# Scores of four heads at once in the last layers of a four-layer cross-attention kernel, and another order on GpSimd in its first layer

## What is computed

```python
q = q.reshape(b, l, KVH, GROUPS, HD).transpose(0, 2, 3, 1, 4)
scores = jnp.einsum('bkgld,bksd->bkgls', q, k) * scale
scores = scores + encoder_attention_mask[:, :, None, :, :]
attn = jax.nn.softmax(scores, axis=-1)
out = jnp.einsum('bkgls,bksd->bkgld', attn, v)
```

## Time and profile before

| | us |
|---|---|
| median of 3 runs | 1202.15 (1202.07 to 1203.07) |
| the profiled execution | 1202.93 |
| its span | 1200.9 |
| granted TensorE clock, mean over the span | 0.983 of full speed |
| layer 0, about | 0 to 702 |
| layer 1, about | 720 to 889 |
| last layers: first turn, last turn | 909.6, 1185.1 |

### The profile page before, as it was taken

How to read it: one execution, slowest core, us unless ns; L and a number is a source line. 1 busy time by engine, 2 the same in 40 slices (tenths; PEclk the granted TensorE clock), 3 DMA queues, 4 the chain that set the end, 5 groups by cost and what they waited for, 6 DMA issues and landing times. The chain is left out here.

```text
span 1200.9 us, 20667 instructions
## 1 busy us (share of the span) xinstructions
PE 1118.7 (93%) x7404; PEld 883.7 (74%) x7404; DVE 808.3 (67%) x1986; ACT 646.7 (54%) x1451; POOL 684.2 (57%) x746
## 2 busy tenths in 40 slices
PE   5999999999999999999999988989689999999996
PEld 4888788988898888898878973444456767667674
DVE  6677666686667766767765757688656655666774
ACT  3655655656556555655565211622235656687764
POOL 3666665675656656656676303476016655565874
PEclk9899999999999999999999997999799999999999
DMA  6101210221022102210220300000020100000000
GB/s 212 55 25 65 71 53 19 71 71 53 19 71 71 54 18 71 71 54 19 71 71 19 93 5 13 1 1 0 1 62 2 37 1 2 1 2 1 11 10 19
DMA packets 35338, 46.97 MB, mean 39 GB/s; under 512 B 3931, under 2 KB 22308, under 8 KB 35237
## 3 DMA queue, kind: packets, MB, share of 16 engines
q1 hardware_dynamic: 34866, 45.00, 11.6%
q10 hardware_dynamic: 370, 0.64, 0.2%
HBM read 44.59 MB, written 1.05 MB: 38 GB/s over the span
## 5 line engine op out<-in xcount | busy, mean ns | idle before, releaser
L379 POOL TENSOR_TENSOR a_prob<-a_prob,a_inv_total 128x512 f32<-128x512 f32 x128 | 144.2, 1126 | 192.4 <-DVE a_inv_total L684 192.4
L2027 POOL TENSOR_TENSOR scores<-scores,neg_max 128x512 f32<-128x512 f32 x144 | 147.5, 1041 | 79.5 <-DVE neg_max L1898 79.3
L574 ACT ACTIVATE a_prob<-psum,a_neg_max 128x257 f32<-128x257 f32 x256 | 119.2, 472 | 101.7 <-DVE a_neg_max L681 100.4
L1821 ACT ACTIVATE prob_T<-psum 128x512 f32<-128x512 f32 x192 | 113.1, 600 | 35.5 <-PE psum L1742 34.0
L1742 PE MATMUL psum<-ident,scores 128*128 128x128 f32 x768 | 117.8, 280 | 1.5 <-POOL scores L2027 1.5
L1742 PEld LDWEIGHTS psum<-ident,scores 128*128 128x128 f32 x768 | 85.7, 141 | 36.8 <-issue 16.3
L1898 DVE CUSTOM_DVE_ANT_0 scores<-psum,ctx_rows 128x256 f32<-128x256 f32 x256 | 93.7, 420 | 18.6 <-PE psum L1742 9.2
L688 DVE TENSOR_TENSOR a_probT_lo<-psum,a_probT_hi 128x512 fp32r<-128x512 f32 x128 | 88.0, 687 | 24.3 <-ACT a_probT_hi L578 24.0
L503 PE MATMUL psum<-ident,a_prob 128*128 128x128 f32 x512 | 77.3, 273 | 14.6 <-POOL rows_bc L383 12.6
L681 DVE TENSOR_REDUCE a_neg_max<-psum 128x2 f32<-128x514 f32 x128 | 87.4, 683 | 1.2 <-PE psum L425 1.2
L503 PEld LDWEIGHTS psum<-ident,a_prob 128*128 128x128 f32 x512 | 60.6, 140 | 32.7 <-DVE a_q_lo L730 13.4
(11 more groups left out here) (358 smaller groups left out, 3319.1 us busy)
## 6 DMA issues: line engine op xcount, KB each, us to landing
wk_raw<-in_L_xattn_wk SPq DMA_DIRECT2D x16, 512.0 KB, 6.3
wq_raw<-in_L_xattn_wq SPq DMA_DIRECT2D x16, 512.0 KB, 5.6
wv_raw<-in_L_xattn_wv SPq DMA_DIRECT2D x16, 512.0 KB, 3.7
wo_raw<-in_L_xattn_wo SPq DMA_DIRECT2D x16, 512.0 KB, 4.0
ctx_rows<-in_ctx SPq DMA_DIRECT2D x3, 512.0 KB, 4.2
x_rows<-in_x SPq DMA_DIRECT2D x2, 512.0 KB, 9.9
ctx_rows<-in_mask_Bx1xSxS_ff SPq DMA_DIRECT2D x1, 1024.0 KB, 5.4
out_dram<-x_rows SPq DMA_DIRECT2D x4, 256.0 KB, 2.1
```

Source lines behind the costliest of these rows:

```text
L379: pool.tensor_tensor(prob[:, m % 4, :, 0:S], prob[:, m % 4, :, 0:S], rtot[:, m % 4, :].unsqueeze(2).to_broadcast([P, 2, S]), ALU.mult)
L574: act.activation(prob[:, m % 4, q, 0:S + 1], s_bank(g)[:, q, 0:S + 1], ACT.Exp, bias=negm[:, m % 4, q:q + 1], accum_out=tot[:, m % 4, q:q ...
L1821: act.activation(pT[:, i % PT, :], t_bank(i), ACT.Exp, scale=1.0 if on_scalar(i) else -1.0).then_inc(exp_ok, 1)
L2027: pool.tensor_tensor(sc[:, i % SC, :, :], sc[:, i % SC, :, :], m[:, i % SC, :].unsqueeze(2).to_broadcast([P, 2, S]), ALU.subtract).then_in ...
```

## The change

- A call of `scores` does the four heads of a quad, in four row groups and four banks. It is issued two quads ahead (`LEAD` = 2), after the turn of each head with i % 4 == 1, and waits until all heads of the quad before have been read by DVE.
- The sums of two quads stand in a row, after every eighth head; for that the probabilities have ten slots instead of eight, and `exp` waits accordingly.
- The values of layer 2 stand 17 columns apart instead of 32; the matmul still loads 32 columns, the last 15 of which belong to the next head. 15 zero columns close each row, and the memset is narrower.
- DVE takes one more maximum ahead of the eviction of a piece behind an odd turn.
- In layer 0, GpSimd does `norm(6)` and `norm(7)` ahead of the wait for V3 and the cut of the value weights in iterations with i % 4 of 1 and 2.

```diff
                     if i % NQ == 2:
                         h_low(event_of(i))
+                    if i % NQ in (1, 2):
+                        norm(6)
+                        norm(7)
                     pool.wait_ge(acc_full, USE[i, 'V3'] + 1)
                     cut_half('v', i + 1, 0)
-                    norm(6)
+                    if i % NQ not in (1, 2):
+                        norm(6)
                     cut_half('v', i + 1, 1)
-                    norm(7)
+                    if i % NQ not in (1, 2):
+                        norm(7)
...
-LEAD = 4
+LEAD = 2
...
-    pe = [('F', p) for p in opening] + [('S', 0), ('S', 1)] + [('F', p) for p in second] + [('S', 2), ('S', 3)]
+    pe = [('F', p) for p in opening] + [('S', 0)] + [('F', p) for p in second] + [('S', 1)]
     for i in range(HEADS):
         pe.append(('T', i))
         if i in behind:
             pe.append(('F', behind[i]))
-        if i % 2 and i // 2 + LEAD < HEADS // 2:
-            pe.append(('S', i // 2 + LEAD))
-        if i % 4 == 1 and i > 4:
-            pe.append(('A', i // 4 - 1))
-    pe += [('A', QUADS - 1)] + [('F', p) for p in ending]
+        if i % 4 == 1 and i // 4 + LEAD < QUADS:
+            pe.append(('S', i // 4 + LEAD))
+        if i % 8 == 1 and i > 8:
+            pe += [('A', i // 4 - 2), ('A', i // 4 - 1)]
+    pe += [('A', QUADS - 2), ('A', QUADS - 1)] + [('F', p) for p in ending]
...
-                    max_to(at + (5 if at % 2 else 6))
+                    max_to(at + 6)
...
-        v_ones2 = sb("v_ones", [P, 2, 4, SMALL[2].KV, 32])
+        v_ones2 = sb("v_ones", [P, 2, 4, SMALL[2].KV * 17 + 15])
...
-        SC, PT = 7, 8
+        SC, PT = 7, 10
...
-        v_ones = {(2, h): v_ones2[:, h] for h in range(2)}
+        v_ones = {(2, h): v_ones2[:, h, :, 0:SMALL[2].KV * 17].rearrange("p t (k e) -> p t k e", e=17) for h in range(2)}
+        v_cols = lambda l, h, t, k: v_ones2[:, h, t, 17 * k:17 * k + 32] if l == 2 else v_ones[l, h][:, t, k, :]
...
-                    l, b, e = head_of(2 * s)
+                    l, b, e = head_of(4 * s)
...
-                    if s >= 2:
-                        pe.wait_ge(s_read, 2 * s - 2)
+                    if s:
+                        pe.wait_ge(s_read, 4 * s)
...
-                            for i in (2 * s, 2 * s + 1):
+                            for i in range(4 * s, 4 * s + 4):
...
                     if i >= PT:
-                        act.wait_ge(a_done, i // 4 - 1)
+                        act.wait_ge(a_done, (i - PT) // 4 + 1)
...
-                    dve.wait_ge(s_full, i // 2 + 1)
+                    dve.wait_ge(s_full, i // 4 + 1)
```

More of the change, by code:

```diff
@@ L1462, in last_layers_orders @@
     for kind, p in pe:
-        if kind == 'S' and p == 2:
+        if kind == 'S' and p == 1:
             act.append(('shift', 2))
@@ L1469, in last_layers_orders @@
             act.append(('keep', p))
-            if p == QUADS - 1:
+            if p == QUADS - 2:
                 at = HEADS
@@ L1713, in scores @@
                 def scores(s):
-                    l, b, e = head_of(2 * s)
+                    l, b, e = head_of(4 * s)
                     sh = SMALL[l]
-                    if s < 2:
+                    if s == 0:
                         pieces = [p for (kind, p), bank in bank_of.items() if kind == 'F' and bank < 4]
                         landed(pe, [max((p for p in pieces if evictor(p) == who), key=number.get) for who in ('act', 'dve')])
-                    if e % 4 == 0 and b % 2 == 0:
+                    if b % 2 == 0:
                         landed(pe, stack_pieces(l, b // 2, e // 4))
-                    if s >= 2:
-                        pe.wait_ge(s_read, 2 * s - 2)
+                    if s:
+                        pe.wait_ge(s_read, 4 * s)
                     at = b % 2 * S
@@ L1756, in sums @@
                             j = i % 4
-                            mm = pe.matmul(a_bank(n)[rows(j), :], v_ones[l, b // 2][:, b % 2 * 2 + t, (e + j) * SMALL[l].KV // SMALL[l].H, :],
+                            mm = pe.matmul(a_bank(n)[rows(j), :], v_cols(l, b // 2, b % 2 * 2 + t, (e + j) * SMALL[l].KV // SMALL[l].H),
                                            pT[:, i % PT, t * S:(t + 1) * S], start=t == 0, stop=t == 1, tile_position=(0, 32 * j))
@@ L1968, in set_ones @@
                     W = SMALL[l].W
-                    pool.memset(v_ones[l, h][:, :, :, W + 1:32], 0.0)
+                    pool.memset(v_ones2[:, h, :, SMALL[2].KV * 17:] if l == 2 else v_ones[l, h][:, :, :, W + 1:32], 0.0)
                     return pool.memset(v_ones[l, h][:, :, :, W:W + 1], 1.0)
```

## The result

The changed kernel takes 1213.43 us in the median of five runs (1212.70 to 1214.76), the kernel before 1202.07 (1200.32 to 1203.07): a ratio of 1.0099, with a 95% interval of 1.0085 to 1.0112, so 11.4 us slower. The forecast was 1205.4, 3.3 slower; the time has its sign and lies in the whole range of 1188 to 1217, but above the 1200 to 1211 that the forecast gave its own mechanism, and the loss is over three times as large as forecast. By the time alone rival B (1211 to 1216) and rival D (1213) would fit too. The question is thus which term was too small.

The account below looks back on a forecast made before the run. PE (TensorE) was taken as the bound, busy 93% of the span. 1202.9 - 7.5 (layer 0) + 9.6 (last layers) + 1.2 (clock) = 1206.2, less 0.8 for the median: 1205.4 us; own range 1200 to 1211, whole 1188 to 1217.

Parts of the forecast that it names:

- rival B: Last layers: half clock costs 1.7 after each of four waits over 2 us, less after nine; 1211 to 1216; chance 0.12.
- rival D: Layer 0: moving GpSimd's normalisations gains nothing; 1213 us; chance 0.10.
- Layer 0: GpSimd's norm(7) ahead of the cuts brings turn T7 1.9 us earlier in four iterations: -7.5 us, bounds 0 and -10.
- What PE no longer does: Last layers: one of two score blocks per quad goes, 29.2 us, paired sums save 5.5: -34.7, plus 0.6 for four-head blocks.
- rival C: Score blocks: row groups run only two at a time, +13 us, 1218 us; chance 0.07.
- The pairs of sums: Last layers: two sum blocks in a row take 1.81, not 2 x 1.00; 0.25 for each of 22 pairs, 5.5 us.
- The waits: Last layers: PE's score blocks of quads 3 to 47 wait for DVE's late maxima, +50.6 us in sum.
- the walk: Last layers: step times of PE and DVE added quad by quad, by slots and order; the layers' sum is +9.6 us.
- The single prices: Score block's wait per quad: 1.15 us plain, 1.55 with one 'OT' piece, 2.9 behind layer 3's projection and moments.
- Rival A: Last layers: only a quad's last maximum is late, wait 0.65 instead of 1.55, 14 us less: 1191 us; chance 0.15.
- the clock: Last layers: four new waits over 2 us can each bring PE to half clock; 0 to 7 us, taken as 1.2.
- The end: From head 182 on, GpSimd's normalisation no longer holds PE up and the last quad's exponential hides behind sums: -2.4 us.

Follow-up runs that it names:

- four blocks later: The changed kernel with only the score blocks of quads 19, 22, 41 and 45 issued one turn later: 1209.40 us, ratio 1.0069 to the kernel before.

## Why the prediction came out as it did

**Layer 0** was right in size and place: 7.5 us forecast, 7.5 measured; T7's time, the unchanged i % 4 == 1 and the cover of about 1 us ahead of norm(0) came as said. Of its signs one came only in part: T7 still waits 0.4 us for GpSimd in two of the four iterations. Rival D (nothing) has the measured time, 1213, but the run with this part alone puts it out.

**What PE no longer does.** The score block of four costs what a pair costs, so rival C is out. The pairs of sums were mis-sized: 0.25 us each was forecast and 0.14 measured, 2.4 us too much for 22 pairs. The pair itself was taken at 1.81 and takes 1.87; the slow turn that was to go with it brought nothing that the traces show.

**The waits.** 50.6 were forecast. The table has 43.8, and 1.0 more at one block that waits for an 'OB' eviction on ScalarE. That is 5.8 less. Some 2.6 of it is the way of counting: the table counts from the modelled end of the last matmul (1127.60 + 1.47 = 1129.07), the walk from the step, 0.07 earlier (1126.67 + 2.33), in 37 places. Another 1.4 was taken by the half clock: the blocks of quads 42 and 46, right behind a stretch, wait 0.13 and 0.54, and 1.05 and 1.06 in the kernel with eight slots, which has no stretch there. The last 1.8 isn't placed. The single prices (1.15, 1.55, 2.9) are met within 0.03 in the table (1.14, 1.52, 2.88). Rival A (only the last maximum late, 0.65 at an 'OT' quad) is out by the 1.52.

**The reason for the waits was half right.** The prediction's first sentence on it says that the slot is free too late. But at an 'OT' quad the three maxima stand behind the eviction in VectorE's written order, and that is the later of the two: an eighth slot took away 2.2 of 44.5 us of waits, nine slots without the order left 39.2, and nine with it 1.7. The walk held both conditions, so its numbers came out; the sentence named only one, and someone who had acted on it would have bought a slot and gained 4.5 us, where the order was worth 31.

**The term that was mis-sized most is the clock.** I took 1.2 us for it, on the ground that VectorE is late anyway while PE runs at half clock, and that only the four waits over 2 us count. Measured are four stretches that cost 5.5 by the walk; between traces, the two in quads 19 to 23 are worth 2.8 and the two in quads 42 to 46 1.8, 4.6 together. The ground was wrong in both halves. VectorE's lateness covers part of a stretch at best: in the second pair 1.4 of 3.2 us of added busy time, as the waits of quads 42 and 46 show, and in the first pair none that shows. And the size of a wait doesn't decide: those of 2.34 in quad 3 and of 2.88 in quad 34 brought none, those of 1.84 and 1.90 in quads 19 and 22 did. Rival B gave the time, 1211 to 1216, with this mechanism, though not with the waits that it named; its 0.12 was too little. That the time came into the whole range is thus owed to the room left for a rival, not to the forecast's own sum.

The rest of the difference: some 3 us are steps that the walk had too short, 2.4 of them the pairs of sums and 0.9 quad 12, ahead of whose block a transposed input and the projection Q behind it wait 0.50 and 0.49 for evictions before them (at 975.26 and 976.81; the second wait was there before the change too). The end gave back 1.2 from head 182 on, not 2.4. With 3.4 of the clock by the traces (4.6 less the 1.2 forecast), or 4.3 by the walk, that makes 7.9 to 8.8 for the 7.9 that the last layers lack; the 1.8 of shorter waits stands against it, and I can't place it closer. Heads 126 to 181 were to take 9 more and took 13.4, some 2 of it clock.

## What to carry to other kernels

Where two engines hand a few buffers to and fro, ask of the late one not how busy it is but what stands in its written order between the event that it could start on and the result that the other waits for. VectorE was busy for 67% of the span and made PE wait 44 us; one line that put the maxima ahead of the evictions turned a loss of 7 us into a gain of 24, in a kernel that had two more slots for it. And where a change makes the bound engine pause every few microseconds, put the clock down as a cost of its own, per stretch from a trace, and not as covered by the wait that stands ahead of it.

## What the runs showed of the hardware

Equal waits don't bring equal clocks. A pause of 2.88 ahead of the same block was followed by half clock within 1.2 us of the block's start in four kernels (eight slots, sums one by one, four blocks later, nine slots without the order), and by full clock in the changed one and in the one with the last layers alone. In the last layers, before their end, a stretch was 3.4 or 6.8 us long, and one of 3.4 cost 0.7 to 1.8 us. The start of the kernel shows it without any edit: iteration 0 took 35.1, 36.0 or 37.4 us with 0, 3.4 or 6.8 us at half clock, the same code each time. The Trainium skill, TensorE: Matmul & The Clock Gate, Part 1, says that the watch on PE's activity runs freely and doesn't start anew with the kernel; the different outcomes behind one wait, and in iteration 0 with the same code, agree with that, but no run here moved one pause alone, so it isn't shown.

A steady pause on the bound engine is easily read as a lack of buffers. The profile gave 36 pauses of 0.3 to 2.9 us, and the eighth slot removed 2.2 us of them. The Trainium skill, Perfetto Trace Analysis, Optimization Strategy, says that consistent bubbles can mean too little SBUF or PSUM for the next tile; here that was true in the smaller part, and the instruction order in the larger.

Four row groups at once cost what two cost: 16 matmuls of 32x256 in 0.74 or 0.75 us in all 16 blocks of layer 2, as 8 did (0.73 or 0.74 once the opening was over).
